# Four edits to a graph network kernel: who compares, in which order, and on which port

## The reference, cut to what matters

```
x = layernorm(x + gcn(x))        # 3 times relu(segment_sum(norm * (x @ W)[src], dst) + b)
x = layernorm(x + attention(x))  # e = sum(leaky_relu(h_l[dst] + h_r[src]) * att); softmax of e over a target's
                                 # edges (segment_max, exp, segment_sum); out = segment_sum(h_r[src] * alpha)
x = layernorm(x + gate(x))       # z = [x[dst], x[src], edge]; segment_sum(sigmoid(z Wf + bf) * softplus(z Ws + bs), dst)
x = layernorm(x + deep(x))       # 10 layers gelu(layernorm(segment_sum(norm * (h @ W)[src], dst) + b)), and a branch
# norm = deg[src]^-1/2 * weight * deg[dst]^-1/2, with a loop on each node
```

## Time and profile before

| what | us |
|---|---|
| median of three executions (3284.44 to 3285.15) | 3285.12 |
| the profiled execution | 3285.47 |
| its span, from the first to the last instruction | 3283.5 |
| TensorE busy | 3106.7 (95%) |
| VectorE busy | 1370.8 (42%) |
| ScalarE busy | 1408.2 (43%) |
| GpSimd busy | 846.8 (26%) |
| mean granted TensorE clock (share of full) | 0.977 |

### The profile page before, as it was taken

The page is one execution under the profiler, slowest core; times in us unless marked ns, Lnnn a source line. Parts: engine busy times, 40 slices in busy tenths (PEclk is TensorE's granted clock), DMA queues, the critical chain, the costliest instruction groups (busy, mean ns, idle before and its releaser), DMA issues. The chain is left out here.

```text
span 3283.5 us, 45208 instructions
## 1 busy us (share of the span) xinstructions
PE 3106.7 (95%) x14568; PEld 2006.1 (61%) x14568; DVE 1370.8 (42%) x3096; ACT 1408.2 (43%) x2506; POOL 846.8 (26%) x939
## 2 busy tenths in 40 slices
PE   7879999979999998999999799999999999999998
PEld 6865555547788775777777555555555555555554
DVE  7971110125666667999999511111111111111112
ACT  6860000225555555888888423333332222222333
POOL 2010000037777763777777000000000000000000
PEclk8989999989999998999999899999999999999999
DMA  2556667723333323666666467666677766777774
GB/s 90 231 236 243 273 282 286 286 61 83 87 83 83 83 70 92 186 194 184 186 185 183 181 288 288 283 284 281 284 287 290 290 281 281 290 291 298 290 298 169
DMA packets 166699, 709.29 MB, mean 216 GB/s; under 512 B 39287, under 2 KB 133090, under 8 KB 153423
## 3 DMA queue, kind: packets, MB, share of 16 engines
q1 hardware_dynamic: 127865, 618.84, 48.5%
q0 software_dynamic: 33600, 83.09, 9.1%
q10 hardware_dynamic: 5011, 4.48, 0.5%
HBM read 657.91 MB, written 48.07 MB: 215 GB/s over the span
## 5 line engine op out<-in xcount | busy, mean ns | idle before, releaser
L1422 PE MATMUL deep_out_psum<-deep_adjacency,deep_scaled_nodes_odd 125*128 125x450 f32 (+1 forms) x1750 | 669.7, 537 | 0.0
L1422 PE MATMUL deep_out_psum<-deep_adjacency,deep_scaled_nodes 125*128 125x450 f32 (+1 forms) x1750 | 669.7, 537 | 0.0
L1670 POOL DMA_INDIRECT source_rows<-gat_source_rows,pair_src x416 | 396.5, 953 | 575.3 <-POOLq L64 448.8
L1422 PEld LDWEIGHTS deep_out_psum<-deep_adjacency,deep_scaled_nodes_odd 125*128 125x128 f32 x1750 | 328.4, 189 | 299.8 <-issue 298.9
L1422 PEld LDWEIGHTS deep_out_psum<-deep_adjacency,deep_scaled_nodes 125*128 125x128 f32 x1750 | 328.1, 189 | 298.9 <-issue 298.0
L2100 POOL DMA_INDIRECT near_room<-gate_source_rows,pair_src x416 | 395.1, 950 | 141.7 <-issue 119.2
L1480 ACT ACTIVATE deep_squares_high<-deep_aggregate,deep_vectors 128x450 fp32r<-128x450 f32 (+1 forms) x70 | 46.7, 668 | 618.1 <-DVE deep_aggregate L1552 618.1
L1422 PE MATMUL gcn_out_psum<-adjacency_columns,gcn_scaled_nodes 125*128 125x450 f32 (+1 forms) x700 | 268.7, 538 | 0.0
L2198 PE MATMUL gate_banks<-edge_weights,edge_features_t 128*128 128x256 f32 x832 | 248.4, 380 | 0.0
L1566 DVE SCALAR_TENSOR_TENSOR deep_normed<-deep_aggregate,deep_vectors,deep_squares 128x450 f32<-128x450 f32 (+1 forms) x70 | 47.9, 684 | 384.9 <-ACT deep_squares L1489 384.9
L1422 PEld LDWEIGHTS gcn_out_psum<-adjacency_columns,gcn_scaled_nodes 125*128 125x128 f32 x700 | 131.2, 190 | 123.5 <-issue 122.8
(11 more groups left out here) (418 smaller groups left out, 4754.0 us busy)
## 6 DMA issues: line engine op xcount, KB each, us to landing
deep_adjacency<-adjacency SPq DMA_DIRECT2D x69, 5625.0 KB, 16.2
adjacency_columns<-adjacency SPq DMA_DIRECT2D x19, 5625.0 KB, 16.1
adjacency<-adjacency_columns SPq DMA_DIRECT2D x7, 5625.0 KB, 17.7
edge_features<-in_edge_attr_dram SPq DMA_DIRECT2D x416, 64.0 KB
att_node_rows<-pair_dst_rows SPq DMA_DIRECT2D x104, 128.0 KB
gate_node_rows<-pair_dst_rows SPq DMA_DIRECT2D x104, 128.0 KB, 3.3
source_rows<-gat_source_rows,pair_src POOLq DMA_INDIRECT x416, 2.5
near_room<-gate_source_rows,pair_src POOLq DMA_INDIRECT x416
```

The source lines that it names most:

```text
L1422: m = nc.tensor.matmul(op[:, n % 2, 0:cols], h[l % 2][:, s, :], ring[0:T, n % 2, s, 0:cols], start=s == 0, stop=s == NS - 1)
L1670: pool.indirect_dma_start(xj[:, b % HOLD, q, :], None, d["h_r"], bass.IndirectOffsetOnAxis(ap=c["pair_src"][:, b * PQ + q:b * PQ + q + 1], ...
```

## The change

1. In **lanes**, the 25 transposes of the features stand ahead of the extra sums in TensorE's stream, and the last transposes wait for one PSUM bank each instead of for all seven copies.
2. In **build**, every third unit (n % 3 == 0) from a block's tenth on has its source one-hots made by GpSimd, three `tensor_scalar` comparisons of 125 columns, and not by VectorE. GpSimd does a block's units before that block's extra edges.
3. In **attention**, from iteration 104 on VectorE does the three steps of the maxima ahead of `message` and `leaky`, and TensorE runs three idle products behind each `scatter`.
4. In **gate**, the turned one-hot becomes a `tensor_tensor` with the lane number broadcast from a PSUM column; `places` hold two steps and not three, so that they are copied every second step; six of the seven folds move to GpSimd, behind its last gather; the last one stays on VectorE; and TensorE runs 16, 8 and 6 idle products of 512 columns around the last two scatters.

```diff
@@ edge_lanes, tensor
             nc.tensor.matmul(p_s[:, 0, 0:GC - 1], nxt[:, 1, :], start[:, 1:GC], start=False, stop=True).then_inc(s_sz, 1)
+            pe.wait_ge(s_lx, 32)
+            for s in range(NS):
+                if s % 4 == 0 and s // 4 >= GC:
+                    pe.wait_ge(s_xc, s // 4 - GC + 1)
+                t = nc.tensor.transpose(p_t[:, s // 4 % GC, s % 4, 0:T], xn[:, s, :], c["ident"][0:T, 0:T])
+                ...
             pe.wait_ge(s_ex, 1)
...
-            pe.wait_ge(s_xc, NXQ)
             for k in range(GC):
+                pe.wait_ge(s_xc, k + (NXQ - 1 - k) // GC * GC + 1)
                 pe.wait_ge(s_fix, k + 1)
@@ build_adjacency
+        POOL_FROM = EXTRA_AT + RING + 2
+        bypool = [n for n, (b, j, u) in enumerate(units) if n % 3 == 0 and j >= POOL_FROM]
...
             for b in range(NSP):
+                for n in (n for n in bypool if units[n][0] == b):
+                    u, k = units[n][2], n % RING
+                    g0, m = u[0], len(u)
+                    if n >= RING:
+                        pool.wait_ge(s_mm, n - RING + 1)
+                    for q in range(m):
+                        i = g.tensor_scalar(ohr[:, k, q, 0:T], c["ramp"][:, 0:T], tab[:, 0, g0 + q:g0 + q + 1], None, ALU.is_equal)
+                    i.then_inc(s_po, 1)
                 lo, hi = bounds(pool, b)
...
-                if n not in byact:
+                if n not in byact and n not in bypool:
...
+                if n in bypool:
+                    pe.wait_ge(s_po, bypool.index(n) + 1)
@@ attention, tensor
+            def keep_busy_behind():
+                pe.wait_ge(s_sc, NSB - 1)
+                for _ in range(FILLERS // 2):
+                    nc.tensor.matmul(p_s[:, NSB % 2, 128:512], rows[:, 0, 0, :], rows[:, 0, 0:3, :].rearrange("r s f -> r (s f)"), start=True, stop=True)
...
+                if NPB <= i < NPB + BEHIND:
+                    keep_busy_behind()
@@ attention, vector
             for i in range(NPB + BEHIND + 1):
+                ends_first = i >= NPB
+                if ends_first and at(i, 2) is not None:
+                    along_lanes(at(i, 2))
+                if ends_first and at(i, 3) is not None:
+                    maxima(at(i, 3))
+                if ends_first and at(i, 1) is not None:
+                    lane_maxima(at(i, 1))
                 if BEHIND <= i < NPB + BEHIND:
                     message(i - BEHIND)
@@ bridge_and_gate, gpsimd
+            for j in range(NSP - 1):
+                c0, n = SPANS[j]
+                pool.wait_ge(s_O, PQ * (DONE[j] + 1))
+                nc.gpsimd.tensor_tensor(c["h_t"][:, c0:c0 + n], c["h_t"][:, c0:c0 + n], odd[:, c0:c0 + n], ALU.add).then_inc(s_fp, 1)
@@ bridge_and_gate, tensor
+            def keep_busy(n):
+                pe.wait_ge(s_et, NPB)
+                for _ in range(n):
+                    nc.tensor.matmul(p_e[:, :], rows[:, 0, 0, 0:128], rows[:, 0, 1:3, :].rearrange("r s f -> r (s f)"), start=True, stop=True)
...
                     core(b + 1)
+                else:
+                    keep_busy(16)
                 if b >= 1:
                     scatter(b - 1)
+            keep_busy(8)
             scatter(NPB - 1)
+            keep_busy(6)
@@ bridge_and_gate, vector
-                vec.tensor_scalar(oht[:, b % 2, :], dr[0:T, b % 4, :], c["lane"][0:T, 0:1], None, ALU.is_equal).then_inc(s_oht, 1)
+                dve.wait_ge(s_pl, b // 2 + 2)
+                vec.tensor_tensor(oht[:, b % 2, :], dr[0:T, b % 4, :], lane.to_broadcast([T, PQ * 128]), ALU.is_equal).then_inc(s_oht, 1)
...
-                if 1 <= b < NPB - 1:
-                    fold(b - 1)
-                if b % 3 == 0 and b + 3 < NPB:
+                if b % 2 and b + 3 < NPB:
                     copy_places(b + 3)
             message(NPB - 1)
-            fold(NPB - 2)
             merge(NPB - 1)
-            fold(NPB - 1)
+            fold_last()
```

More of the change, by code:

```diff
@@ L269, in _ @@
             nc.tensor.matmul(p_s[:, 0, 0:GC - 1], nxt[:, 1, :], start[:, 1:GC], start=False, stop=True).then_inc(s_sz, 1)
+            pe.wait_ge(s_lx, 32)
[3 more added lines that the diff above has]
+                t = nc.tensor.transpose(p_t[:, s // 4 % GC, s % 4, 0:T], xn[:, s, :], c["ident"][0:T, 0:T])
+                if s % 4 == 3 or s == NS - 1:
+                    t.then_inc(s_xt, 1)
             pe.wait_ge(s_ex, 1)
@@ L276, in _ @@
             m.then_inc(s_sm, 1)
[L277 to L283, removed]
             pe.wait_ge(s_of, 1)
@@ L402, in build_adjacency @@
                  "distances_ready", "far_onehots_ready", "sixes_ready", "members_marked", "marks_ready", "degrees_summed", "degree_step", "degree_guarded", "degree_root", "dinv_ready", "dinv_turned",
-                 "dinv_copied")
+                 "dinv_copied", "pool_onehots_ready")
         (s_p, s_oh, s_mm, s_ev, s_om, s_oo, s_omm, s_oc, s_od, s_blk, s_loc, s_dg, s_xs, s_xp, s_xl, s_xv,
-         s_af, s_ao, s_t6, s_mb, s_mk, s_d, s_v, s_in, s_rt, s_n, s_t, s_c) = (c["sems"].take("build_" + n) for n in names)
+         s_af, s_ao, s_t6, s_mb, s_mk, s_d, s_v, s_in, s_rt, s_n, s_t, s_c, s_po) = (c["sems"].take("build_" + n) for n in names)
         s_st = c["adj_stored"]
@@ L1978, in _ @@
                     leaky(i - 1)
-                if at(i, 2) is not None:
+                if not ends_first and at(i, 2) is not None:
                     along_lanes(at(i, 2))
-                if at(i, 3) is not None:
+                if not ends_first and at(i, 3) is not None:
                     maxima(at(i, 3))
@@ L1986, in _ @@
                     carried(at(i, 4))
-                if at(i, 1) is not None:
+                if not ends_first and at(i, 1) is not None:
                     lane_maxima(at(i, 1))
@@ L2056, in bridge_and_gate @@
         p_e, p_a = banks[:, 0, :], banks[:, 1, :]
-        places = banks[:, 1, PQ * T:PQ * T + 3 * PQ]
+        places = banks[:, 1, PQ * T:PQ * T + 2 * PQ]
+        lane = banks[0:T, 1, PQ * T + 2 * PQ:PQ * T + 2 * PQ + 1]
         p_z = banks[:, 2:8, :].rearrange("p (k a) c -> p k a c", k=CORES)
@@ L2072, in bridge_and_gate @@
                  "core_sum", "core_sum_read", "core_abs", "core_exp", "log", "softplus", "gate", "messages", "pair_sums", "node_sums", "columns_summed",
-                 "places_copied")
-        (s_w, s_wn, s_cl, s_oh, s_oht, s_eT, s_et, s_z, s_zr, s_ab, s_ex, s_ln, s_sp, s_gt, s_msg, s_A, s_O, s_fin, s_pl) = (
+                 "places_copied", "first_columns_summed")
+        (s_w, s_wn, s_cl, s_oh, s_oht, s_eT, s_et, s_z, s_zr, s_ab, s_ex, s_ln, s_sp, s_gt, s_msg, s_A, s_O, s_fin, s_pl, s_fp) = (
             c["sems"].take("gate_" + n) for n in names)
@@ L2103, in _ @@
                 pool.wait_ge(s_g[b % 4], 16 * PQ * (b // 4 + 1))
+            for j in range(NSP - 1):
+                c0, n = SPANS[j]
+                pool.wait_ge(s_O, PQ * (DONE[j] + 1))
+                nc.gpsimd.tensor_tensor(c["h_t"][:, c0:c0 + n], c["h_t"][:, c0:c0 + n], odd[:, c0:c0 + n], ALU.add).then_inc(s_fp, 1)
+            pool.wait_ge(s_fp, NSP - 1)
         @block.sync
@@ L2354, in copy_places @@
             def copy_places(b):
-                n = min(3, NPB - b) * PQ
+                n = 2 * PQ
                 if b:
@@ L2363, in onehots @@
                     dve.wait_ge(s_z, b - 1)
-                vec.tensor_scalar(oht[:, b % 2, :], dr[0:T, b % 4, :], c["lane"][0:T, 0:1], None, ALU.is_equal).then_inc(s_oht, 1)
+                dve.wait_ge(s_pl, b // 2 + 2)
+                vec.tensor_tensor(oht[:, b % 2, :], dr[0:T, b % 4, :], lane.to_broadcast([T, PQ * 128]), ALU.is_equal).then_inc(s_oht, 1)
                 if b >= 4:
                     dve.wait_ge(s_A, b - 3)
-                dve.wait_ge(s_pl, b // 3 + 1)
-                place = places[:, b % 3 * PQ:(b % 3 + 1) * PQ]
+                place = places[:, b % 2 * PQ:(b % 2 + 1) * PQ]
                 vec.tensor_tensor(oh[:, b % 4, :, :], c["ramp"][:, 0:T].unsqueeze(1).to_broadcast([128, PQ, T]),
@@ L2399, in merge, with fold_last @@
                     vec.tensor_tensor(o, o, p_a[:, q * T:(q + 1) * T], ALU.add).then_inc(s_O, 1)
[L2401 to L2407, removed]
+            def fold_last():
+                c0, n = SPANS[NSP - 1]
+                dve.wait_ge(s_O, PQ * (DONE[NSP - 1] + 1))
+                vec.tensor_tensor(c["h_t"][:, c0:c0 + n], c["h_t"][:, c0:c0 + n], odd[:, c0:c0 + n], ALU.add).then_inc(s_fin, 1)
+                dve.wait_ge(s_fin, 1)
             normed(0)
@@ L2428, in _ @@
                 if i == 7:
+                    vec.tensor_copy(lane, c["lane"][0:T, 0:1]).then_inc(s_pl, 1)
                     copy_places(0)
@@ L2431, in _ @@
                     onehots(i - 7)
+                if i == 8:
+                    copy_places(2)
             for g in range(NG_ + 1):
```

## The result

The changed kernel takes 3298.5 us (median of 6, 3296.0 to 3300.6), the kernel before in the same comparison 3284.8 (3283.9 to 3286.5): ratio 1.004, 95% interval 1.0029 to 1.0051, slower. The forecast was 3290.2, range 3280 to 3298; half a microsecond above its upper end, and on the slow side as two in five of the chances had it. The profiled execution took 3300.6 with a span of 3298.6, so its parts add up to +15.1 against the profile before, 1.4 more than the medians. Two of the chips that the experiments ran on are slower, with the kernel before in 3795 and 3712 us and TensorE's granted clock at 0.73 to 0.77 in attention where it is 0.96 here, so conclusions from the runs there (b_compare, b_build, b_tail, b_lanes, b_build2, b_tail2) rest only on what lies ahead of attention.

A forecast was written before the change was run, and what follows sets the result against it. GpSimd's gathers were taken to set the gate's step at 5.00 us, VectorE after the change. Terms +18.5 -2.2 -1.0 +0.3 -7.5 -0.5 -2.5 = +5.1 gave 3290.6, or 3290.2 on the median's scale; range 3280 to 3298.

The forecast's parts named there:

- Gate, compare: Gate loop: compare takes 0.67 us, VectorE's step 5.18 passes GpSimd's 5.00; +19.3 less 0.8 for a short first step, +18.5.
- Gate, folds and tail: Gate's end: folds beside VectorE's last steps save 1.3 us, last scatter at high clock with idle products 0.9; together -2.2.
- The next stage's first products: Stage after the gate: its first products should start at the high clock, -1.0 us, between 0 and -2.
- Build: Build: store chain sets the period; five blocks lose 1.9 us each, sixth and seventh nothing, 9.5 in all, taken as -7.5.
- Rival 2: Build: port contention between GpSimd's new comparisons and VectorE's one-hots takes the 7.5 us gain back, 3297.7; chance 0.15.
- Rival 4: Build: the stage isn't held by the store chain and gives 12 us, 3285.7; chance 0.15.
- Lanes: Lanes: copies begin some 4 us earlier, extra sums some 4 us later with VectorE's corrections behind them; -0.5 us.
- Attention's tail: Attention's tail: new order gives 0, idle products keep the clock up for scatters, -2.5 us, between -5 and +2.
- rival 3: Attention's tail: the clock falls all the same, idle products delay scatters, +2 in place of -2.5, 3294.7; chance 0.10.
- Ahead of the gate's loop: Before the gate's loop: two longer compares and one more copy cost +0.3 us.
- rival 1: Gate: compare costs no more than 0.5 us, GpSimd's pace stays, the 18.5 us vanish, 3271.7; chance 0.10.
- the 0.41: Whole kernel: chance of a slower result, made up of rivals 2 and 3 and a third of the prediction's own case.

The follow-up runs named there:

- b_compare: Kernel before with only the gate's compare against the lane column in PSUM (places in two halves), slower chip: 3769.9 us against 3795.1, ratio 0.9957.
- b_build: Kernel before with the build part alone, 37 units' one-hots on GpSimd: ratio 0.9984 (0.9946 to 1.0021).
- b_tail: Kernel before with attention's tail alone, maxima first and three idle products for each of the last steps: ratio 0.9985 (0.9939 to 1.003).
- b_lanes: Kernel before with lanes' part alone, features turned ahead of the extra sums: ratio 0.9984 (0.9949 to 1.0018).
- b_build2: Same kernel as b_build, the kernel before with the build part alone, on another chip: ratio 0.9959 (0.9919 to 0.9999).
- b_tail2: Same kernel as b_tail, the kernel before with attention's tail alone, on another chip: ratio 0.9983 (0.995 to 1.0017).
- the fastest kernel: Changed kernel with the compare on SBUF operands again and no GpSimd drain at the end of the gate's block: 3265.8 us, ratio 0.994.

## Why the prediction went as it did

By its own steps, with the shifts of the profiled execution:

- **Gate, compare, +18.5.** Right: +19.4. The 0.67 is 0.679, the 5.18 is 5.18, GpSimd waits for `add`. What it hid: the 514.2 of before held 2.5 us of folds, which the change removes too. With the folds on the same engine on both sides the compare lengthens the loop by 21.5 (on VectorE) or 22.6 (on GpSimd), and moving the folds gives 2.1 to 2.5; only their net was in my term, and that the two nearly met is luck. The 0.8 for a short first step wasn't there.
- **Gate, folds and tail, -2.2.** From last addition to last fold 14.0 became 12.0 us: -2.0, right (1.5 of it with the folds alone, so some 0.6 for the idle products, where I had 1.3 and 0.9). But the step "if they ran late they would cost one addition, 1.1 us" is the one that failed. I asked what folds on GpSimd would do to VectorE, and not what GpSimd did at that time before: a drain of 8.55 us, which lay beside the last messages. Behind the folds it costs +5.9 (the gap from last fold to next stage, 1.95 to 7.9 us). It is the largest miss of the sum.
- **The next stage's first products, -1.0.** Nothing. They run at half clock as before: the greatest of these products (L1024) is 1.12 us, as it was before (L1012 there). And it isn't the drain's fault alone: without it the last fillers end at 1845.8, TensorE waits 3.4 us for its next operand, and the clock is at 0.50 again at 1850; in the fastest kernel the first product is quick and the next 4 us run at 0.57. The gain of a high clock at the start is lost a little later in the same stage.
- **Build, -7.5.** Right in sum: -7.7 in this trace (the last store's 9.3 less the 1.6 of lanes), -6.6 between the stores with build alone. The store chain was the bound, not the engines: 37 units left VectorE, 14.5 us of its busy time, and half of that came through. The split was less right: the six periods lost 1.7, 2.2, 1.0, 1.3, 0.8 and 0.4 us, where I had 1.9 in each of the first and nothing in the last two. Rival 2 was seen and was small: VectorE's one-hots (L505) have a median of 0.539 and a greatest of 0.67; GpSimd's comparisons reach 1.31 at a median of 0.60. (Of the two stretched rows that this rival started from, one had lost 0.17 us and the other 0.49, not both 0.17.) Rival 4 fell: it wanted 12.
- **Lanes, -0.5.** -1.6 here. The corrections behind the extra sums came 1.8 us later, not 4, and ended when they had before (27.8 us).
- **Attention's tail, -2.5.** -1.4 here, -1.3 to -2.5 over all traces. The clock was full from 1218 to 1232 and fell once more, to 0.50, when TensorE had stood idle for 1.0 and 1.8 us around two short products, waits that the fillers don't bridge. So rival 3 held for a few microseconds only.
- **Ahead of the gate's loop, +0.3.** +1.0, within what this stretch varies by (54.3 to 57.6 us).

So the mechanism that carries the result, VectorE in GpSimd's place as the gate's bound, was right in kind and size, and rival 1 is refuted. That "slower" had 0.41 is no merit of the prediction: it came through the drain, which was in none of the cases that made up the 0.41. The sum was 8.6 us short by the medians (+13.7 for +5.1) and 10 by the profiled executions; of these 10, 5.9 are the drain, 1.0 the clock that doesn't last, 1.1 attention's tail, 0.9 the compare and 0.7 the stretch ahead of the loop, and lanes' 1.1 go the other way; the 1.5 that remain are under 1 in each of GCN, attention's steps and the last stage, and none is assigned to an edit.

## What to carry to other kernels

An engine freed from a wait can be slowed by the cure: the compare's waiting (0.34 us without, 0.497 on the mean with it) cost nothing while the other engine set the pace, and its 0.679 us in the new form cost 22 us over 104 steps; compare the two engines' cycles before trading one for the other. Before work is given to an engine that looks idle at a stage's end, look into its sequencer's queue: drains and barriers are not counted as busy. And when two parts of a change work on one loop, measure each against the loop without the other.

## What was not expected of the hardware

GpSimd's drain at the end of the gate's block, behind 832 gathers, took 8547 ns in each of eight kernels, on the slower chips too, and 40 ns when another had gone before it with six additions between. At the end of build, where five gathers of the lanes stage lie behind it and no block of gathers, it was 1677 ns. Nothing shows it as busy time, and the other kind of drain behind the block took 0.23 to 0.26 us whether this one had gone before or not.
